# A stage for measurement behind the second loop of a two-layer graph network: 216 gathers beside copies by ACT and products by TensorE

## What is computed

```python
# layer 0
msg  = relu(concat([x[dst], x[src], edge_attr, u[0]]) @ W1 + b1)
agg  = segment_sum(msg, dst)
x    = layernorm(x + relu(concat([x, agg, u[0]]) @ W2 + b2))
# layer 1
Z    = einsum('ni,rio->nro', x, fc_weight)
z_s, z_d = Z[src, etype], Z[dst, etype]
e    = relu(sum(concat([z_s, z_d]) * attn_weight[etype]))
alpha = softmax of e over the edges with the same dst
x    = layernorm(x + segment_sum(alpha * z_s, dst))
```

## Time and profile before

| what | us |
|---|---|
| median of 2 executions | 5615.59 (5615.11 to 5616.06) |
| the profiled execution, its own time | 5665.02 |
| the profiled execution, its span | 5663.3 |

### The profile page before, as it was taken

The page is one execution under the profiler, slowest core; times in us unless marked ns, Lnnn a source line. Parts: engine busy times, 40 slices in busy tenths (PEclk is TensorE's granted clock), DMA queues, the critical chain, the costliest instruction groups (busy, mean ns, idle before and its releaser), DMA issues. The chain is left out here.

```text
span 5663.3 us, 70822 instructions
## 1 busy us (share of the span) xinstructions
PE 3303.8 (58%) x17849; PEld 2900.7 (51%) x17849; DVE 2986.9 (53%) x9486; ACT 1277.2 (23%) x4180; POOL 3023.9 (53%) x3265
## 2 busy tenths in 40 slices
PE   2265555555555554555893076666666666666676
PEld 1264444444444444444761065555555555555575
DVE  1265544555455544554873065555555555555567
ACT  0100000000000000000021044444444444444455
POOL 5625555555555555555116706666666666666631
PEclk5555555555555555555566555555555555555555
DMA  3211111111111111111134101111111111111111
GB/s 114 82 43 51 45 52 44 51 53 45 52 44 50 53 45 52 51 45 53 51 123 147 35 25 46 46 46 46 47 46 46 46 46 46 46 47 46 46 35 31
DMA packets 172540, 300.13 MB, mean 53 GB/s; under 512 B 71720, under 2 KB 78236, under 8 KB 158845
## 3 DMA queue, kind: packets, MB, share of 16 engines
q0 software_dynamic: 100032, 105.03, 9.5%
q1 hardware_dynamic: 70662, 188.25, 9.4%
q10 hardware_dynamic: 1462, 2.30, 0.1%
HBM read 260.36 MB, written 34.99 MB: 52 GB/s over the span
## 5 line engine op out<-in xcount | busy, mean ns | idle before, releaser
L453 POOL DMA_INDIRECT ring<-Btab,idx x1563 | 1480.6, 947 | 1247.9 <-DVE XA L846 642.6
L453 POOL DMA_INDIRECT ring<-Ztab,idx x1563 | 1476.2, 944 | 957.1 <-issue 405.9
L732 PE MATMUL p_s<-msg,oh 128*128 128x64 f32 x3328 | 778.3, 407 | 679.9 <-issue 639.3
L732 PEld LDWEIGHTS p_s<-msg,oh 128*128 128x128 f32 x3328 | 748.3, 326 | 670.2 <-issue 669.9
L1342 PE MATMUL p_s<-ring,ohx 128*128 x3328 | 812.3, 422 | 177.5 <-issue 174.5
L1342 PEld LDWEIGHTS p_s<-ring,ohx 128*128 128x128 f32 x3328 | 740.3, 327 | 196.5 <-issue 196.4
L719 PE MATMUL p_m<-A,oht 128*128 x1664 | 435.9, 366 | 574.1 <-DVE full L853 537.0
L830 DVE TENSOR_TENSOR oh<-p_i,dstl 128x1024 f32<-128x1024 f32 x208 | 253.5, 1219 | 941.1 <-remote 826.6
L1316 PE MATMUL p_ei<-S,oht 128*128 x1664 | 325.3, 198 | 684.0 <-issue 627.0
L632 ACT ACTIVATE msg<-p_t 128x512 f32<-128x512 f32 x208 | 124.2, 597 | 2579.5 <-issue 1987.4
L719 PEld LDWEIGHTS p_m<-A,oht 128*128 128x128 bf16 x1664 | 237.1, 144 | 696.4 <-issue 653.9
(11 more groups left out here) (211 smaller groups left out, 3191.0 us busy)
## 6 DMA issues: line engine op xcount, KB each, us to landing
drow<-drow_d SPq DMA_DIRECT2D x104, 1024.0 KB
eaT<-in_eaT_in SPq DMA_DIRECT2D x208, 128.0 KB
Ztab<-Z_stage SPq DMA_DIRECT2D x49, 536.0 KB, 5.4
ring<-Btab,idx POOLq DMA_INDIRECT x1563
ring<-Ztab,idx POOLq DMA_INDIRECT x1563
xTB<-in_xTB_in SPq DMA_DIRECT2D x7, 448.0 KB
Btab<-B_stage SPq DMA_DIRECT2D x7, 448.0 KB, 6.8
ring<-in_xTA_in SPq DMA_DIRECT2D x7, 448.0 KB
```

What stands on the lines that cost most here:

```text
L453: e.indirect_dma_start(out=ring[:, place(t), :], out_offset=None, in_=table[:, :], in_offset=bass.IndirectOffsetOnAxis(ap=idx[:, t:t + 1], ...
L732: last = e.matmul(pS[r % 2][:, j, :], OH[:, r % QO, j, :], msg[:, r % 2, j, :], start=True, stop=True)
```

## The change

A new phase, `phase_measure`, is called between `phase_layer1` and `phase_out`. It has three lists of instructions and one semaphore, `s_clock`, between two of them.

- ACT: 11 stretches (`len(SEGMENTS) + 2`) of 320 activations (`REST * 2`), Copy, each of 128x32 f32 from the constant `A.ident` to a slot of its own in `seen`. The last of a stretch raises `s_clock`, and ACT waits for that before it begins the next stretch.
- POOL: nine stretches of 24 indirect DMAs, each stretch begun when ACT has ended one more of its own, and ended by a wait until all 24 have landed. The forms: 128 rows (twice), 120, 124, 64 and 126 rows, 128 single words, and 128 rows with one or with three memsets of 128x24 behind each DMA.
- TensorE: 2500 products of bf16 128x128 by 128x128 into one bank, with no wait.

```diff
+SEGMENTS = [("rows", 128), ("rows", 120), ("rows", 124), ("rows", 64), ("word", 128), ("fill", 128), ("fill2", 128), ("rows", 126), ("rows", 128)]
+EACH = 24
+REST = 160
+
+def phase_measure(nc, A):
+
+    with ExitStack() as ctx:
+        sem = lambda n: ctx.enter_context(nc.semaphore(n))
+        sb = lambda n, s, d: ctx.enter_context(nc.sbuf_tensor(n, s, d))
+        spare = sb("spare", [P, EACH, ZW], F32)
+        small = sb("small", [P, 4, EACH, 24], F32)
+        seen = sb("seen", [P, 2 * REST, 32], F32)
+        pV = bank(ctx, nc, "pv", [P, P])
+        s_ms, s_clock = sem("measure_gathered"), sem("measure_clock")
+        words = A.Ztab.rearrange("a b -> (a b)").unsqueeze(1)
+        block = ctx.enter_context(nc.Block())
+
+        @block.gpsimd
+        def _(e):
+            for i, (kind, n) in enumerate(SEGMENTS):
+                e.wait_ge(s_clock, i + 1)
+                for k in range(EACH):
+                    if kind == "word":
+                        e.indirect_dma_start(out=spare[0:n, k, 0:1], out_offset=None, in_=words,
+                                             in_offset=bass.IndirectOffsetOnAxis(ap=A.idx1[0:n, k:k + 1], axis=0)).then_inc(s_ms, 16)
+                    else:
+                        e.indirect_dma_start(out=spare[0:n, k, :], out_offset=None, in_=A.Ztab[:, :],
+                                             in_offset=bass.IndirectOffsetOnAxis(ap=A.idx1[0:n, k:k + 1], axis=0)).then_inc(s_ms, 16)
+                    for m in {"fill": (0,), "fill2": (1, 2, 3)}.get(kind, ()):
+                        e.memset(small[:, m, k, :], 0.0)
+                e.wait_ge(s_ms, 16 * EACH * (i + 1))
+
+        @block.scalar
+        def _(e):
+            for i in range(len(SEGMENTS) + 2):
+                if i:
+                    e.wait_ge(s_clock, i)
+                for k in range(REST * 2):
+                    ins = e.activation(seen[:, k, :], A.ident[:, 0:32], ACT.Copy)
+                ins.then_inc(s_clock, 1)
+
+        @block.tensor
+        def _(e):
+            for i in range(2500):
+                e.matmul(pV, A.ident_h[:, :], A.iota_h[:, :], start=True, stop=True)
+
@@
         phase_mid(nc, A)
         phase_layer1(nc, A)
+        phase_measure(nc, A)
         phase_out(nc, A)
```

## The result

The changed kernel takes 6188.46 us (6187.85 to 6189.07, 2 runs) beside 5615.59 before: a ratio of 1.1018, 95% interval 1.0992 to 1.1045. It is 572.9 us slower, where 419.6 were forecast, and lies outside the range. The direction was right; 153 us are missing from the sum.

What follows compares the result with a forecast made beforehand. No engine was full; two long loops stay unchanged. The new phase adds its longest list, ACT's 419.6 us, with POOL and TensorE hidden: 5615.6 + 419.6 = 6035.2 us, range 6022 to 6064, chance 0.84.

Steps and rivals of the forecast that it cites:

- ACT's term: New phase: 3520 copies, one every 0.1187 us, 417.8 us; with waits, tail and second meeting 419.6 us.
- The seam: Between second loop and output phase all engines meet, so the new phase is added whole, at its slowest engine's length.
- So I put all of POOL at 0, hidden by ACT's copies: New phase: POOL's gathers add 0, at 32 us a stretch beside ACT's 38.1.
- POOL's term: New phase: nine stretches of 24 gathers, 32 us each, counted as 0; without ACT's cover 290 us.
- the five rivals: POOL last 6068 us (0.05); slower copies 6093 (0.05); memory operand 6364 (0.02); TensorE last 6336 (0.02); lists dropped 5616 (0.02).
- two named POOL and TensorE: Rivals on which engine ends the new phase: POOL, 6068 us, chance 0.05; TensorE, 6336 us, chance 0.02.
- TensorE's 2500 products: New phase: one product every 0.108 us, 270 us at the lower clock, less at the upper, hidden inside 419.
- Rival 1's rule: Gathers use the largest DMA-engine count up to 16 dividing their partitions; rival: POOL ends last, 6068 us, chance 0.05.

Runs made afterwards that it cites:

- e1: Changed kernel with its 216 gathers left out, copies and products kept: 4614.55 us, where the kernel before took 4191.12.
- e2b: Changed kernel with 20 gathers a stretch and a wait for landing every 4: 6039.72 us, ratio 1.0751 to the kernel before at 5618.00.
- again: Changed kernel rerun unchanged: 6190.93 us, ratio 1.1022 to the kernel before at 5616.90.
- again2: Changed kernel rerun unchanged once more: 6192.03 us, ratio 1.1021 to the kernel before at 5619.86.
- e7b: Kernel before plus 14 stretches varying gather pace, rows and copy width, where it takes 5619.86 us; no total given, plain 128-row gathers lose 18.7 us.
- e5: Kernel before plus 14 stretches varying gather form, waits and engines beside, where it takes 5616.90 us; no total given, 24 unbroken gathers cost 18.7 us.
- e7: Same plan of 14 stretches varying gather pace, rows and copy width, where the kernel before took 4195.37 us: 4843.94 us.

## Why the prediction was wrong

**ACT's term was right.** The spacing forecast was 0.1187 us, the measured stretches of e1 are 38.31 to 38.40 us, wait included, which is 0.1194, and the stage without gathers adds 423.4 us against 419.6. The Trainium skill's figures ("ScalarE: Activation LUTs", section "What ACT_TABLE_LOAD costs") gave 0.1197 us; the measured 0.1194 agrees with them within 0.3%. The seam was right as well: L1536, the first instruction of the output phase, begins 0.3 us after the last copy, released by a sequencer.

**The step that failed is "So I put all of POOL at 0, hidden by ACT's copies".** It took "hidden" for a question of lengths: 32 us of POOL beside 38 of ACT. POOL is in fact the shorter one. But where the kernel before takes 5616 us, gathers issued every 1.25 us without a pause are followed by ACT, DVE and TensorE standing still for most of the time, for ACT from some 9 us after the first gather when it is alone, and from 5 to 6.5 us with a second busy engine. Eight stretches lose 148.4 us so. The proof by undoing: the stage with pauses (and 20 gathers a stretch, not 24) adds 421.7 us there (e2b), against 572 to 574 without (again, again2).

**The bounds of POOL's term were missing, not just its value.** The forecast allowed POOL to be late, never to be dear for others. None of the five rivals has this mechanism, though two named POOL and TensorE; each asked which engine ends last. TensorE's 2500 products, forecast at 270 us or less, needed 245, with 82 us of idle time of the same kind in them. That they stayed inside the forecast is luck. It was summed at the lower level of the clock, and the granted clock was 0.94 in the first stretch, mostly the upper one, which the forecast had named as possible; without gathers, at 0.98, they take 141.8 us (e1). With them the clock fell too. TensorE's products first stop at 5619.8, 3 us after the first gather, and the granted clock goes from 1.00 (5616 to 5620) to 0.50 (5624 to 5628).

**The profile of before held a sign of it.** I did not read it. Two groups of TensorE, kernel before:

```profile
L732 PE MATMUL p_s<-msg,oh 128*128 128x64 f32 x3328 | 778.3, 407 | 679.9 <-issue 639.3
...
L1316 PE MATMUL p_ei<-S,oht 128*128 x1664 | 325.3, 198 | 684.0 <-issue 627.0
```

The same two in e1, whose loops are the same code, where the kernel before takes 4191 us:

```profile
L732 PE MATMUL p_s<-msg,oh 128*128 128x64 f32 x3328 | 758.1, 422 | 50.2 <-ACT msg L632 47.2
...
L1316 PE MATMUL p_ei<-S,oht 128*128 x1664 | 321.0, 200 | 27.6 <-DVE oht L1380 25.7
```

1266 us of idle time that waits for nothing stood on the page. The label alone is not safe: in the profile of the changed kernel, whose first loop is as long within 30 us, L732 has 117.9 us of "issue", and 1043.4 us stand at L719 as a wait for DVE. The idle time of these two, L719 and L1321 together is steadier, 1953 us before and 1928 after, against 721 in e1. It also ends with the gathers: steps of the second loop in the timeline of the kernel before, beside gathers (the first two rows) and after the last gather at 5448 us (the last two):

```profile
4489.02 0.21 ACT L1283 ACTIVATE ex<-ed 128x8 f32<-128x8 f32 x1 [6.94 <-DVE ed L1438]
...
4500.95 0.21 ACT L1283 ACTIVATE ex<-ed 128x8 f32<-128x8 f32 x1 [6.90 <-DVE ed L1438]
...
5486.69 0.21 ACT L1283 ACTIVATE ex<-ed 128x8 f32<-128x8 f32 x1 [3.21 <-DVE ed L1438]
...
5495.06 0.21 ACT L1283 ACTIVATE ex<-ed 128x8 f32<-128x8 f32 x1 [3.36 <-DVE ed L1438]
```

11.9 us a step beside gathers, 8.4 without. Eight gathers need 10 us, so POOL alone doesn't explain 11.9: it had been waiting 2.2 us a step for the others, and they for what nobody shows. In e1 the 1563 gathers of this loop are out in 1957 us, 1.25 each; in the kernel before they took 2423. These rows would have said that gathers cost the others something. They would not have given its size in the stage, since only 1.9 of the 11.9 us are over POOL's own pace.

**Rival 1's rule.** The 124-row gathers lasted 1.28 us and not 0.94, and came every 1.59. They made no stretch longer. The Trainium skill ("DMA: Bandwidth & Descriptors", section "Why a DMA increments its semaphore by 16 and not by 1") has 4 DMA engines for 124 partitions, 15 for 120 and 14 for 126. The packets in the traces agree with the three counts: a gather of 120 rows is 15 packets of 8 rows, one of 126 rows 14 packets of 9, one of 124 rows four of 16 and four of 15. And no form made POOL end last. But the forecast had 124 rows issued every 1.25 us, as the others. Their slower pace is enough to spare ACT, as e7b shows with 128 rows at 1.43 and 1.49.

## What to carry to other kernels

"Hidden beside" needs two tests: is it shorter, and does it leave the others their pace. Idle time released by "issue" on several engines at once, which ends when one engine's stream ends, is a reason to suspect that stream; slow it or break it up, and see, before counting it as free. A producer that runs in bursts ahead of need can be slowed: here a memset of 310 columns behind each gather brought the whole kernel 11.5%. But measure the kernel before beside it each time, since the same change costs 18% where nothing is held up.

## What the runs showed of the hardware that was not expected

- The same kernel before takes 4191 to 4195 us in two sets of runs and 5616 to 5620 in three and at the start. In the first kind 24 and 48 unbroken gathers hold nobody up; in the second 24 do so in the stage, and the loops are held up too. The record numbers the chips: 5 and 3 for the first kind, 0, 15 and 13 for the second, none of them twice. So it may belong to the chip, but no run tells that from anything else that changed with it.
- In the blocked time single copies of ACT mostly start 0.70 or 1.40 us apart. The gathers themselves aren't slowed: they go on every 1.25 us. Nor do they land late: by the packets in the traces the 24 gathers of 128 rows begin to move 1.6 us behind the first issue and are done 2.1 us behind the last where ACT is blocked (e5, e7b), and 1.6 and 2.3 us where it isn't (e7). So it is no backlog of their transfers.
- The loss beside ACT alone is 6.2 us at a gather every 1.39 us and gone at 1.49 (and at 1.43, with a pause of POOL in it); with DVE and TensorE beside it is 7.0 us at 1.49.
- What runs up and blocks the issue stays open. It isn't bytes or rows, nor DMAs as such (plain ones from POOL every 0.53 us are free), nor POOL's memsets. The record gives a span and a granted clock for every run of the experiments, so each of them seems to have been watched by the profiler. Whether the same time is lost where nobody watches, or whether what runs up are the profiler's own records of instructions and DMAs, no run here tells. Loading of instructions that comes late was argued against, not tested: in the trace of the changed kernel the packets of ACT's instruction queue stay 128 copies apart through the blocked stretch (after 294, 422 and 550 copies).
